# Node chunks of the last phase of a graph network kernel: seven of 896 nodes, or ten of three sizes

## What is computed

```
x  = layernorm(x + L0(x))
Wh = x @ W + b
sim[e]  = cosine(Wh[row[e]], Wh[col[e]])
base[e] = adj_v[e] * softplus(deg_coeff[0] * deg_v[e] + deg_coeff[1]) * (row[e] != col[e])
prop_pos[n] = sum over e with row[e] == n of base[e] * relu(sim[e]) * Wh[col[e]]
prop_neg[n] = the same with -relu(-sim[e])
out = layernorm(x + scale * (c0 * prop_pos + c1 * prop_neg + c2 * Wh))
```

## Time and profile before

| | us |
|---|---|
| runs | 4663.32, 4669.24, 4670.95 (median 4669.24) |
| profiled execution | 4667.63 |
| its span, first to last instruction | 4666.1 |
| first instruction of `last_rows` (POOL gather) | 3294.0 |
| last row added (L1421) | 4312.5 |
| last unit blended (L1404) | 4643.1 |

### The profile page before, as it was taken

How to read it: one execution, slowest core, us unless ns; L and a number is a source line. 1 busy time by engine, 2 the same in 40 slices (tenths; PEclk the granted TensorE clock), 3 DMA queues, 4 the chain that set the end, 5 groups by cost and what they waited for, 6 DMA issues and landing times. The chain is left out here.

```text
span 4666.1 us, 63774 instructions
## 1 busy us (share of the span) xinstructions
PE 3164.4 (68%) x16285; PEld 1891.2 (41%) x16285; DVE 3103.2 (67%) x5138; ACT 1589.8 (34%) x3302; POOL 3235.3 (69%) x3224
## 2 busy tenths in 40 slices
PE   4576777777767776776555555565477767677888
PEld 3344445444545444444334444443233232322222
DVE  6776767767776777774655555554377866576787
ACT  3422323223332323233421221221354544454444
POOL 0577777777777777775477777777576777776546
PEclk7888888888888889887777777777698989799899
DMA  3332323333332333232322222222355645455556
GB/s 63 120 93 91 100 87 98 91 91 98 94 97 89 98 90 99 89 98 83 111 72 66 79 70 66 81 68 67 112 159 147 175 133 159 122 156 152 174 172 194
DMA packets 355302, 502.08 MB, mean 108 GB/s; under 512 B 93127, under 2 KB 214984, under 8 KB 354809
## 3 DMA queue, kind: packets, MB, share of 16 engines
q1 hardware_dynamic: 251689, 394.52, 26.0%
q0 software_dynamic: 100352, 102.96, 10.7%
q10 hardware_dynamic: 2896, 0.59, 0.1%
HBM read 290.63 MB, written 207.16 MB: 107 GB/s over the span
## 5 line engine op out<-in xcount | busy, mean ns | idle before, releaser
L835 POOL DMA_INDIRECT frows<-messages,fidx x2352 | 2285.2, 972 | 831.5 <-issue 669.3
L915 PE MATMUL fps_b<-hot_key,hot_lo 128*128 128x343 f32 x3136 | 1235.0, 501 | 418.7 <-PEq L71 413.0
L974 DVE TENSOR_TENSOR strip<-strip,fps_b 128x343 f32 x1568 | 788.1, 503 | 541.6 <-DVEq L71 527.2
L850 ACT ACTIVATE turned<-fps_t 128x512 f32<-128x512 f32 (+1 forms) x754 | 431.9, 573 | 1750.9 <-ACTq L71 1748.0
L905 PE MATMUL fps_sum<-hot,frows 128*64 128x80 f32 x4704 | 550.0, 301 | 601.2 <-PEq L71 601.2
L1161 POOL DMA_INDIRECT lrows<-messages,lidx x784 | 744.6, 950 | 287.0 <-issue 221.6
L915 PEld LDWEIGHTS fps_b<-hot_key,hot_lo 128*128 128x128 f32 x3136 | 540.6, 206 | 743.2 <-issue 696.3
L905 PEld LDWEIGHTS fps_sum<-hot,frows 128*64 128x64 f32 x4704 | 521.9, 195 | 694.0 <-issue 694.0
L944 DVE TENSOR_SCALAR hot_key<-iota_f,edge 128x343 f32<-128x343 f32 x1574 | 753.4, 479 | 0.2
L1351 ACT ACTIVATE pos<-l_c,coeff 128x896 f32<-128x896 f32 x392 | 394.1, 1006 | 491.0 <-PE l_c L1222 490.2
L1222 PE MATMUL l_c<-unit_t,unit_g 64*128 64x448 f32 x1568 | 428.9, 624 | 159.3 <-DVE acc L1150 91.6
(11 more groups left out here) (192 smaller groups left out, 1983.4 us busy)
## 6 DMA issues: line engine op xcount, KB each, us to landing
adj<-turned SPq DMA_DIRECT2D x696, 256.0 KB
edge<-adj SPq DMA_DIRECT2D x294, 448.0 KB
adj_x<-adj SPq DMA_DIRECT2D x98, 448.0 KB
frows<-messages,fidx POOLq DMA_INDIRECT x2352, 2.4
messages<-msg SPq DMA_DIRECT2D x14, 1120.0 KB, 4.6
lrows<-messages,lidx POOLq DMA_INDIRECT x784
adj<-turned SPq DMA_DIRECT2D x58, 64.0 KB
wh_g<-wh_rows SPq DMA_DIRECT2D x56, 32.0 KB, 1.7
```

The source lines that it names most:

```text
L835: pool.indirect_dma_start(rows[:, q, k, :], None, tab_l[l].ap(), bass.IndirectOffsetOnAxis(ap=idx[:, q, k:k + 1], axis=0)).then_inc(s_got[ ...
L850: act.activation(turned[j][:, 0:(b - a) * P], ps_t[j][:, 0:(b - a) * P], ACT.Copy).then_inc(s_t_free, 1)
L915: pe.matmul(ps_b[n % KB][:, 0:NT * TWIN], hot_lo[:, s % 2, k, :], hot_key[:, n % KB, :], start=True, stop=True).then_inc(s_b, 1)
L974: dve.tensor_tensor(part, part, ps_b[n % KB][:, 0:NT * TWIN].rearrange("p (h w) -> p h w", w=TWIN), ALU.add).then_inc(v, 1)
```

## The change

The chunks are given by BOUNDS in tiles. The first four stay as they were; the last 21 tiles are cut 4, 3, 4, 3, 4, 3, so that there are ten chunks, which end at 9, 10, 11, 12, 13, 14 blocks. `needs` becomes 0, 0, 0, 9, 19, 25, 35, 41, 51, 56, and `READY` 3, 7, 11, 15, 17, 19, 21, 23, 25, 28. Chunks of at most four tiles have no second half, so four of the 19 steps drop out (`xt1`, `xk1`, `ut1`, `uk1`). After the chunks that end at an odd number of blocks (save the last but one) only the newly complete block is visited; the older blocks catch up in the next chunk (`upto`). Blocks 12 and 13 are treated as all others in the closing stages, so the last `out` adds `out_t` too, and a memset clears block 13 of it. The closing stages keep 896 nodes each. OWN and PARTS stay.

```diff
+            BOUNDS = (0, 7, 14, 21, 28, 32, 35, 39, 42, 46, 49)
+            NC = len(BOUNDS) - 1
+            SIZE = [hi - lo for lo, hi in zip(BOUNDS, BOUNDS[1:])]
+            BLOCKS = [P * hi // SB for hi in BOUNDS[1:]]
+            READY = [(P * hi - 352) // 224 + 1 for hi in BOUNDS[1:-1]] + [PAIRS]
+            HALVES = [((0, 4), (4, n - 4)) if n > 4 else ((0, n),) for n in SIZE]
+            HB = [sum(len(k) for k in HALVES[:c]) for c in range(NC + 1)]
...
-            for c in range(NCH):
+            upto = [0] * NSB
+            for c in range(NC):
                 first_of.append(len(units))
-                for b in range(2 * c + 2):
-                    ps = range(before[c] if b < 2 * c else 0, READY[c])
+                for b in range(BLOCKS[c]):
+                    if BLOCKS[c] % 2 and c < NC - 2 and b < BLOCKS[c - 1]:
+                        continue
+                    ps = range(upto[b], READY[c])
+                    upto[b] = READY[c]
                     visits.append((b, len(units), len(units) + len(ps) - 1))
                     units += [(b, p) for p in ps]
...
-            needs = [max(0, 16 * (c + 1) + 1 - first_row) if c < NCH - 1 else n_rows for c in range(NCH)]
+            needs = [max(0, -(-P * BOUNDS[c + 1] // SLOPE_ROW) + 1 - first_row) if c < NC - 1 else n_rows for c in range(NC)]
...
-            chain = [(c, step) for c in range(NCH) for step in STEPS]
+            chain = [(c, step) for c in range(NC) for step in STEPS if SIZE[c] > 4 or step not in ("xt1", "xk1", "ut1", "uk1")]
...
                             for j in range(CH):
-                                if c < NCH - 1:
-                                    pe.matmul(ps_h[:, j * F:(j + 1) * F], out_t[:, (c * CH + j) * P:(c * CH + j + 1) * P], eye2[:, :], start=True, stop=False)
+                                pe.matmul(ps_h[:, j * F:(j + 1) * F], out_t[:, (c * CH + j) * P:(c * CH + j + 1) * P], eye2[:, :], start=True, stop=False)
...
                     def layer2(c):
-                        i = tiles(c)
+                        i, m = part(c), SIZE[c]
+                        if c == NC - 1:
+                            dve.memset(out_t[:, (NSB - 1) * SB:NSB * SB], 0.0).then_inc(s_zero, 1)
```

More of the change, by code:

```diff
@@ L1366, in _ @@
                                 act.wait_ge(s_var, c + 1)
[L1367 removed]
+                                act.activation(mom[:, 2, part(c)], mom[:, 1, part(c)], ACT.Sqrt).then_inc(s_std, 1)
                             elif step in ("xk0", "xk1"):
                                 half = int(step[2])
[L1370 to L1371 removed]
+                                lo, n = HALVES[c][half]
+                                act.wait_ge(s_xt, HB[c] + half + 1)
                                 act.activation(xt[:, lo * P:(lo + n) * P], ps_h[0:F, 0:n * P], ACT.Copy).then_inc(s_xk, 1)
@@ L1374, in _ @@
                                 act.wait_ge(s_sq, c + 1)
-                                act.activation(mom[:, 3, tiles(c)], mom[:, 0, tiles(c)], ACT.Sqrt).then_inc(s_nrm, 1)
+                                act.activation(mom[:, 3, part(c)], mom[:, 0, part(c)], ACT.Sqrt).then_inc(s_nrm, 1)
                             elif step in ("uk0", "uk1"):
                                 half = int(step[2])
-                                act.wait_ge(s_ut, 2 * c + half + 1)
+                                act.wait_ge(s_ut, HB[c] + half + 1)
                                 if c == 0 and half == 0:
@@ new lines, in add_sums, with spread, turned, centre @@
+                        dve.tensor_tensor(sums, sums, ps_sum[0:F, 0:WIN], ALU.add).then_inc(s_add, 1)
+                    def spread(ap, m):
+                        return ap.rearrange("p (i o) -> p i o", o=1).to_broadcast([P, m, F])
+                    def turned(m):
+                        return ps_h[:, 0:m * F].rearrange("p (c f) -> p c f", f=F)
+                    def centre(i, m, s_done):
+                        a, b = t1[:, 0:m, :], t2[:, 0:m, :]
+                        link(dve.tensor_reduce(mom[:, 0, i], a, AX.X, ALU.add))
@@ L1438, in layer @@
-                        link(dve.tensor_tensor(t1[:, :, :], t1[:, :, :], x_sb[:, i, :], ALU.add))
-                        centre(i, s_var)
+                        link(dve.tensor_tensor(t1[:, 0:m, :], turned(m), skip[:, i, :], ALU.add))
+                        link(dve.tensor_tensor(t1[:, 0:m, :], t1[:, 0:m, :], x_sb[:, i, :], ALU.add))
+                        centre(i, m, s_var)
                     def layer2(c):
-                        i = tiles(c)
+                        i, m = part(c), SIZE[c]
```

88 lines of the change are left out of this document (41 added, 47 removed).

## The result

The changed kernel takes **4620.43 us** (median; 4618.10 to 4625.17) where the kernel before, on the same chip, takes 4666.93 (4663.32 to 4670.95): a ratio of 0.9899, 95% interval 0.9886 to 0.9912. The forecast was 4640 with a range of 4620 to 4677, so the sign was right, the time lies at the range's low end, and the gain is 46.5 us where 27.3 were forecast. The question of this study is where the other 19 came from.

What follows compares the result with a forecast made beforehand. Gathers were taken to bound late rows, PE the stage behind. Rows +6.9, units -37.1, last chain -10.8, carries +11.3, end +1.8 and +0.6 sum to -27.3: from 4667.63 to 4640 us, range 4620 to 4677.

Steps and rivals of the forecast that it cites:

- what bounds the stages: Late in the rows POOL's gathers bound and time is free; behind the rows PE bounds, at 1.86 us a unit.
- units and carries: Behind the rows: 20 fewer units, 37.1 us less; twelve carries at 0.94 us of PE, 11.3 more.
- the chains: Each chunk's serial steps: 16.3 us for four tiles, 13.9 for three; the last chain behind the rows 10.8 less.
- rival A: Chains in the rows don't shrink, at 25.1 us each through order of waits and granted clock: 4700, slower; chance 0.13.
- I keep 53.6 for six: The six closing stages between units behind the rows keep their 53.6 us; bound: 2 us more each.
- PE is the bound: Behind the rows cosine groups follow with products between and no gap, so PE sets 1.86 us a unit.
- B: Chains at 18.2 to 21.3 us, or dearer carries and closing stages with chains at 17: about 4667; chance 0.15.
- C: Chains of 8 us fit the rows' free time, last add at 4312.9: 4628; on the forecast's side, together 0.72.
- D: Rows stay empty because a chunk's chain ends too late for its units; given no chance.

Runs made afterwards that it cites:

- e10_after_again: The changed kernel run once more without edits: 4620.05 us, 0.9887 of the kernel before.
- e1_after_swap: The changed kernel with POOL multiplying the even units behind the rows and DVE the odd ones: 4639.8 us, 0.9924 of the kernel before.
- e3_before_busy: The kernel before with six more PE matmuls, into a bank nobody reads, two units after each closing stage's beginning: 4672.36 us, ratio 1.0002.
- e2_before_swap: The kernel before with DVE's and POOL's units behind the rows swapped: 4664.95 us against 4672.44, ratio 0.9983.
- e8_skip_last: The changed kernel with the last chunk but one also visiting only its new block, so no carries behind the rows: 4613.36 us, 0.9878 of the kernel before.
- e11_skip_again: The kernel of e8_skip_last run once more, on the same chip as the changed kernel's repeat: 4607.76 us, 0.9869 of the kernel before.

## Why the prediction was right and wrong

**Right: what bounds the stages.** Late in the rows the gathers were the bound and time there was free. ACT's wait for gathers, 69.1 us before, is gone from the waits of 3800 to 4320, the time is filled with 20 units, and nothing stalls behind row 14. Plain rows take 15.19 where 15.2 was said.

**Right: units and carries.** Behind the rows 116 units remain. Each of the twelve carries costs 0.94, the price of the one row that showed it. PE's matmul groups have the records forecast for carries, 88 (two groups, for the two banks):

```profile
L1253 PE MATMUL l_o<-sums_t,ident 128*128 128x448 f32 x76 | 40.8, 620 | 1.6 <-ACT sums_t L1352 1.0
...
L1253 PE MATMUL l_sum<-sums_t,ident 128*128 128x448 f32 x12 | 7.0, 665 | 0.0
```

**Right in kind, a little high: the chains.** Scaling chunk 0's pieces gave 16.3 and 13.9; measured are 14.4, 14.0 and 15.5 for four tiles, 14.3 and 14.5 for three. Together 72.7 against 76.7, 4.0 of the rows' 4.3 us (in e10_after_again the five make 74.9). Three tiles cost what four do, which scaling by width doesn't give. The steps do shrink: from the add that chunk 4 waits for (row 18, 3682.34) to its first transposes there are 8.17 us, from that of chunk 5 (row 24, 3787.84) 7.69. But the first load of rows is issued 31.06 and 31.12 us behind the add: what the narrower chunk gains in its steps is lost waiting for its turn among the units. That much of rival A, the order of waits, is in the short chains too. The last chain makes units wait 11.1 where 13.9 was said. The gap in its middle answers the earlier trace rows:

```profile
4335.66 0.90 PE L1272 MATMUL l_h<-ident,both 128*128 128x128 f32 x3 [2.59 <-DVE both L1502]
4336.49 1.87 PE L1234 MATMUL l_c<-unit_t,unit_g 64*128 64x448 f32 x4
```

2.59 us in place of 7.17, though the cosines behind it still take 1.87, at a granted clock of 0.50. Part of that is the block again, `mom<-mom` at 0.25 in place of 2.04, and not the width.

**Wrong: the closing stages.** The failed step is the sentence "I keep 53.6 for six". It treats the price of a stage as a property of the stage. I weighed only whether six units leave room for the disturbance, and bounded the step on one side, 2 us more each. It was -14.8, three quarters of the 19.2 by which the sum was off. The price depends on which engine multiplies the unit ahead of the stage, and the new list happens to turn that around: the stages are 8.8 to 9.1 us in every kernel where it is POOL, 6.3 to 6.5 in every one where it is DVE, with ten units between or with six, and 7.5 with the first blocked instruction taken out. The list could have told it: before, the first stage follows unit 289, the 34th behind the rows and so POOL's; after, unit 334, the 59th and so DVE's. Nothing in the change aims at that, so this part of the gain is luck. With the units swapped back, in e1_after_swap, where a stage costs what the forecast held fixed, the change gains 27.9 us in the three phases, against the 27.3 forecast. "PE is the bound" was right for the units and wrong within the stages, where DVE set the pace. The profile of before had the clue: the same 128x448 operation at 2.16 inside the stages and at 0.62 at the very end. That duration held a wait that no line shows, and I took it for work.

The Trainium skill describes this on its page "SBUF — State Buffer", section "Who interferes with whom": a DVE instruction with two inputs in SBUF contends with a GpSimd instruction that reads SBUF, the one that issues first holds the shared ports for its whole length, and one with a single SBUF input doesn't contend outside VectorE's two-port modes. The trace agrees where it can show it: 2.50 against 0.67 and 2.16 against 0.62 behind a POOL multiply, the multiply 2.85 against 2.07 behind a DVE multiply, and DVE's blend, which takes one input from PSUM, 1.15 with POOL at work. The blocked `mom<-mom`, with one input, would have to fall under that exception; which mode an instruction ran in no trace shows. That the ports are the cause is the Trainium skill's account; the runs show who blocks whom and for how long.

**The rivals.** *A* (chains stay at 25) fell at the first chain, 14.4. The short chain's gap was still followed by half the clock (0.50, the 1.87 above), but the granted clock behind the rows rose, 0.96 against 0.93. The Trainium skill's page "TensorE: Matmul & The Clock Gate", section "HAM oscillation — how this bites in real kernels", by which many short stalls could cost more than few, did not decide here: e3_before_busy took the falls away in the closing stages and gained nothing, because PE was not the bound in them. *B* fell with it. *C* (rows at the gathers' floor) needed chains of 8 us and fell with the 14.0 to 15.5 measured, though the last add comes only about 3 us behind that floor: 22.7 us after the last gather's start, where it was 20.7 before, and 4318.27 in a trace that began 2.1 later. *D* fell: the adds run at full rows.

**Not settled:** the 6.8 us ahead of the first stage in e2_before_swap, of which blocked chain steps and a late `adj` load show only a part; the longer end of e8_skip_last and e11_skip_again; and the 3.1 us by which row 10 came later in code that the change leaves alone, which lies within the 16 us that the first gather moves between traces.

## What to carry to other kernels

A cost that is read as "so much for each" holds only as long as what stands beside it stays; when a change moves an instruction against work that alternates between engines, ask which neighbour it gets. Compare the durations of one operation at one shape over the whole trace: here 0.62 and 2.16 us of the same DVE work differed by a wait that no view lists. And a slow clock, or an idle engine, is a price only where that engine is the one that ends last.

## What the hardware showed that was not expected

- A DVE operation of 128x448 with both inputs in SBUF takes 0.62 to 0.67 us alone, and up to 2.50 when it begins 0.84 us into a POOL multiply of 128x896; it ends 0.48 to 0.49 us after POOL does, whether it began 0.84 or 1.90 into the multiply.
- A DVE operation with one input tensor of 128x7 takes 2.04 us when it begins 0.84 into such a multiply, and ends 0.02 after it; the same step at 128x3 takes 0.25 when it begins 0.23 before the multiply's end, and 0.15 in the rows, where POOL multiplies nothing.
- The reverse holds too: a POOL multiply of 128x896 takes 2.07 us when it begins 0.17 ahead of such a DVE instruction, and 2.85 when DVE's multiply of 1.08 began 0.16 ahead.
- With the granted clock at 1.00 in place of 0.93 over 156 us, and PE busy for 151 of them, the kernel's time was the same to 0.1%.
